# Two-layer graph network: order of the first stage's products, and who fills the gate's bias and the masks into PSUM

## The reference

```
h = relu(layernorm(x))                                   # layer 0, 12 heads of 32
v = h @ W                      ; th = tanh(v)
s = leaky(th . w_src + (th . w_dst)^T, 0.2) ; s = -999 where not adj ; p = softmax(s)
f = elu(p @ v + b)             ; g = sigmoid(h @ H_w.T + H_b)
x = x + g * f + (1 - g) * h
h = relu(layernorm(x))                                   # layer 1, 6 heads of 64
q, k, v = h @ Wq + bq, h @ Wk + bk, h @ Wv + bv
x = x + softmax(q k^T / 8 + (0 or -9e15 by adj)) @ v @ Wf + bf
```

## Time and profile before

| | |
|---|---|
| device time, median of 3 runs | 1072.71 us (1072.68 to 1074.22) |
| the profiled execution's own time | 1072.87 us |
| its span | 1070.8 us |
| busy: PE | 991.1 us (93%), 10153 matmuls |
| busy: DVE | 780.3 us (73%) |
| busy: ACT | 574.5 us (54%) |
| busy: POOL | 277.7 us (26%) |
| chain that ended last | PE 55%, DVE 27%, ACT 7%, issue 7% |

### The profile page before, as it was taken

One profiled execution on the slowest core, in us unless ns is written; L12 is line 12 of the kernel. 1 busy time (PEld: TensorE's weight loads), 2 busy tenths in 40 slices (PEclk: granted clock), 3 DMA queues, 4 the chain that ended last, 5 costly groups with the idle time before them and its releaser, 6 DMA issues.

```text
span 1070.8 us, 24885 instructions
## 1 busy us (share of the span) xinstructions
PE 991.1 (93%) x10153; PEld 857.0 (80%) x10153; DVE 780.3 (73%) x1456; ACT 574.5 (54%) x1126; POOL 277.7 (26%) x338
## 2 busy tenths in 40 slices
PE   6589999999999999999999999999999999999686
PEld 5487878888787887978788797878879788887575
DVE  4867867778786777868677886767788676876814
ACT  6556466373746636374564638446463754745331
POOL 2233140502415051240504124050321406032120
PEclk9689999999999999999999999999999999999988
DMA  9211151510414142031413204151241515111102
GB/s 237 32 15 20 29 90 32 90 32 31 61 32 91 31 82 40 31 62 32 91 32 77 41 12 83 31 91 31 65 39 19 91 32 90 32 47 18 28 30 59
DMA packets 183652, 56.41 MB, mean 53 GB/s; under 512 B 164978, under 2 KB 183540, under 8 KB 183540
## 3 DMA queue, kind: packets, MB, share of 16 engines
q1 hardware_dynamic: 183540, 54.83, 28.3%
HBM read 17.06 MB, written 12.58 MB: 28 GB/s over the span
## 4 chain that ended last, share of the span: by engine, by line
PE 55%; DVE 27%; ACT 7%; issue 7%; POOL 0%; ACTq 0%; DVEq 0%; POOLq 0%
PE ps L624 11%; PE ps L610 10%; PE ps L626 10%; PE ps L625 10%; DVE x L948 5%; PE ps L693 5%; PE ps L790 4%; DVE ee L945 4%; ACT p L430 3%; DVE hT1l L1056 3%; DVE hT0l L858 3%; DVE stats L842 3%; DVE p L973 2%; PE ps L808 2%; DVE x_in L996 2%
## 5 line engine op out<-in xcount | busy, mean ns | idle before, releaser
L410 POOL TENSOR_TENSOR x_in<-x_in,ee 128x384 f32<-128x384 f32 x64 | 72.5, 1134 | 626.7 <-DVE ee L951 626.7
L469 ACT ACTIVATE th<-ps 128x384 f32<-128x384 f32 x64 | 31.9, 499 | 209.8 <-DVE v_tok L936 209.8
L1020 DVE TENSOR_TENSOR hT1l<-ps,hT1h 128x512 fp32r<-128x512 f32 x48 | 30.4, 685 | 88.2 <-ACT hT1h L540 88.1
L984 DVE COPY_PREDICATED_SCALAR z<-not_adj,masked 128x768 f32 x64 | 69.4, 1084 | 32.5 <-ACT z L501 32.5
L610 PE MATMUL ps<-ident,p 128*128 128x128 f32 x576 | 76.3, 283 | 17.8 <-ACT p L430 10.0
L403 POOL TENSOR_TENSOR x_in<-x_in,h 128x384 f32<-128x384 f32 x64 | 85.5, 1367 | 18.5 <-DVE Wf_lo L883 18.5
L610 PEld LDWEIGHTS ps<-ident,p 128*128 128x128 f32 x576 | 65.3, 144 | 23.0 <-issue 12.7
L624 PE MATMUL ps<-Wf_hi,hT1h 128*128 128x384 f32 x192 | 69.0, 359 | 10.4 <-DVE hT1l L1056 10.4
L397 POOL TENSOR_TENSOR x_in<-x_in,bf_row 128x384 f32<-128x384 f32 x64 | 62.1, 1003 | 48.0 <-ACT p L430 48.0
L507 ACT ACTIVATE z<-z 128x768 f32<-128x768 f32 x64 | 54.5, 853 | 28.1 <-DVE z L989 28.0
L501 ACT ACTIVATE z<-ps 128x384 f32<-128x384 f32 x128 | 52.5, 497 | 31.0 <-PE ps L693 31.0
(11 more groups left out here) (130 smaller groups left out, 2796.5 us busy)
## 6 DMA issues: line engine op xcount, KB each, us to landing
V<-v_tok SPq DMA_DIRECT2D x128, 192.0 KB, 5.0
x_in<-in_x_dram SPq DMA_DIRECT2D x16, 768.0 KB, 5.0
out_dram<-x_in SPq DMA_DIRECT2D x16, 768.0 KB, 3.6
x<-in_L_gnn_H_w_dram SPq DMA_DIRECT2D x1, 576.0 KB, 5.9
QT<-in_L_gnn_W_dram SPq DMA_DIRECT2D x3, 192.0 KB, 6.7
thT<-in_L_gnn_Wq_dram SPq DMA_DIRECT2D x1, 576.0 KB, 5.8
z<-in_L_gnn_Wk_dram SPq DMA_DIRECT2D x1, 576.0 KB, 6.8
z<-in_L_gnn_Wv_dram SPq DMA_DIRECT2D x1, 576.0 KB, 7.9
```

The source lines that it names most:

```text
L410: pool.tensor_tensor(x_in[:, i % 3, t], x_in[:, i % 3, t], ee[:, t], ALU.subtract).then_inc(x2_made, 1)
L984: dve.copy_predicated(zt, not_adj[:, t].unsqueeze(1).broadcast_to((P, HEADS0, N)), masked0[:].unsqueeze(2).broadcast_to((P, HEADS0, N))).t ...
```

## The change

- RING begins with the four th_made jobs, then the four gate_tanh jobs, so W0's four products stand in banks 0 to 3 and the gate's in banks 4 to 7. PE makes all W0 products first, then all gate products.
- From i = 2 on ACT copies the broadcast bias (a new tile hb_all, loaded by a new DMA) into the gate's banks, and PE accumulates on it, without the bias matmul.
- In i = 1 to 15 ACT copies the masks into the score banks, and PE's mask matmuls are gone.
- DVE's values0 of the next group move from the head of an iteration to the end of the one before, between the closing steps; those of group 0 stand ahead of the loop, with the late weights' low parts between them. add_out(0) moves ahead of close(2), add_out(1) ahead of close(3).
- ACT's th_and_gate is split, and normalise1 has three th and gate pairs ahead of it instead of two, with the last gate tanh behind it.

```diff
-        pairs_of_jobs = zip(jobs("th_made", 0, th_made, 4), jobs("gate_tanh", 0, gate_tanh, 4))
         RING = (
-            [x for pair in pairs_of_jobs for x in pair]
+            jobs("th_made", 0, th_made, 4)
+            + jobs("gate_tanh", 0, gate_tanh, 4)
...
+        def bias_by_act(i):
+            return real(i) and real(i - 2)
+        def mask_by_act(i):
+            return real(i) and real(i - 1)
...
+            sp.dma_start(hb_all[:], H_b.rearrange("(a e) -> a e", a=1).broadcast_to((P, D))).then_inc(consts_loaded, 16)
...
+                def put_bias(t):
+                    if bias_by_act(i):
+                        act.wait_ge(*last_reader(i, job("gate_tanh", t)))
+                        act.activation(ps[:, job("gate_tanh", t) % BANKS, 0:D], hb_all[:], ACT.Copy).then_inc(bias_put, 1)
+                def put_mask(q):
+                    if mask_by_act(i):
+                        pair = q // 2
+                        act.wait_ge(mask1_made, j + 1)
+                        act.wait_ge(*last_reader(i, job("scores1_shifted", q)))
+                        act.activation(ps[:, job("scores1_shifted", q) % BANKS, 0:D].rearrange("p (t k m) -> p t k m", t=2, m=N),
+                                       mask1[:, 2 * pair:2 * pair + 2].unsqueeze(2).broadcast_to((P, 2, PAIRS1, N)), ACT.Copy)\
+                            .then_inc(mask_put, 1)
...
                     for t in range(TILES):
                         toks = slice(t * P, (t + 1) * P)
                         take(i, job("th_made", t))
+                        if not real(j) and t == TILES - 1:
+                            pe.wait_ge(small_ready, 3)
                         product(ps[:, job("th_made", t) % BANKS, 0:D], lambda c: hT0h[:, c, toks], lambda c: hT0l[:, c, toks],
                                 lambda c: wh["W0"][:, c], lambda c: wl["W0"][:, c]).then_inc(values0_full, 1)
-                        take(i, job("gate_tanh", t))
+                    for t in range(TILES):
+                        toks = slice(t * P, (t + 1) * P)
                         dst = ps[:, job("gate_tanh", t) % BANKS, 0:D]
+                        if bias_by_act(i):
+                            pe.wait_ge(bias_put, TILES * (i - 2) + t + 1)
+                            product(dst, lambda c: hT0h[:, c, toks], lambda c: hT0l[:, c, toks],
+                                    lambda c: wh["Hw"][:, c], lambda c: wl["Hw"][:, c], begun=True).then_inc(gate_full, 1)
+                        else:
...
                 def scores(pair):
+                    if mask_by_act(i):
+                        pe.wait_ge(mask_put, TILES * j + 2 * pair + 2)
...
                 if real(j):
-                    pe.wait_ge(mask1_made, j + 1)
-                    masks()
+                    if not mask_by_act(i):
+                        pe.wait_ge(mask1_made, j + 1)
+                        masks()
```

More of the change, by code:

```diff
@@ L519, in exp_elu @@
                         act.activation(ee[:, t], x1[:, t], ACT.Exp, bias=minus1[:]).then_inc(elu_exp, 1)
-                th_and_gate(0)
-                th_and_gate(1)
+                put_bias(0)
+                tanh_values(0)
+                put_bias(1)
+                tanh_values(1)
+                tanh_gate(0)
+                put_bias(2)
+                tanh_values(2)
+                tanh_gate(1)
+                put_bias(3)
+                tanh_values(3)
+                tanh_gate(2)
                 if real(j):
                     normalise1(j)
-                th_and_gate(2)
-                th_and_gate(3)
+                tanh_gate(3)
                 if real(i):
@@ L568, in body @@
                 copy_k(2)
+                for q in range(4):
+                    put_mask(q)
                 exp0(3)
@@ L617, in take, with product @@
                 return ps[:, at % BANKS]
[L619 removed]
+            def product(dst, left_h, left_l, right_h, right_l, more=False, begun=False, chunk_ready=None):
                 for c in range(C):
@@ L623, in product @@
                         pe.wait_ge(*chunk_ready(c))
-                    pe.matmul(dst, left_h(c), right_h(c), start=(c == 0), stop=False)
-                    pe.matmul(dst, left_h(c), right_l(c), start=False, stop=False)
-                    mm = pe.matmul(dst, left_l(c), right_h(c), start=False, stop=(c == C - 1 and not more))
+                    pe.matmul(dst, left_h(c), right_h(c), start=(c == 0 and not begun), stop=False, skip_group_check=begun)
+                    pe.matmul(dst, left_h(c), right_l(c), start=False, stop=False, skip_group_check=begun)
+                    mm = pe.matmul(dst, left_l(c), right_h(c), start=False, stop=(c == C - 1 and not more), skip_group_check=begun)
                 return mm
@@ L902, in source_dest_consts, with values0 @@
                 dve.wait_ge(sd_consts, 2)
+            def values0(g, t):
+                if real(g):
+                    dve.wait_ge(values0_full, TILES * g + t + 1)
+                    if g == 0 and t == 0:
+                        dve.wait_ge(small_ready, 5)
+                    if real(g - 2) and t == 0:
+                        dve.wait_ge(values1_spread, 64 * (g - 1))
+                    dve.tensor_tensor(v_tok[:, t].rearrange("p (h e) -> p h e", e=E0),
+                                      ps[:, job("th_made", t) % BANKS, 0:D].rearrange("p (h e) -> p h e", e=E0),
+                                      b0_plus1[:].unsqueeze(1).broadcast_to((P, HEADS0, E0)), ALU.add)\
+                        .then_inc(values0_made, 1)
+            for t in range(TILES):
+                values0(0, t)
+                late_lows(t)
+            source_dest_consts()
             def body(i, par):
@@ L1062, in body @@
                 close(1)
+                add_out(0)
                 close(2)
-                add_out(0)
+                values0(i + 1, 0)
+                add_out(1)
+                values0(i + 1, 1)
                 close(3)
-                add_out(1)
                 stats_of_x2(0)
@@ L1069, in body @@
                 add_out(2)
+                values0(i + 1, 2)
                 stats_of_x2(2)
@@ L1074, in body @@
                 add_out(3)
+                values0(i + 1, 3)
             iterations(dve, body)
```

51 lines of the change are left out of this document (16 added, 35 removed).

## The result

| | before | after |
|---|---|---|
| device time, median of 4 runs | 1073.06 us (1072.68 to 1074.22) | 1047.21 us (1046.33 to 1047.84) |
| the profiled execution, its span | 1072.87 us, 1070.8 us | 1046.33 us, 1044.4 us |
| busy: PE | 991.1 us (93%), 10153 matmuls | 968.0 us (93%), 10037 matmuls |
| busy: DVE | 780.3 us (73%) | 775.1 us (74%) |
| busy: ACT | 574.5 us (54%) | 630.1 us (60%) |

The ratio is 0.9757 (0.974 to 0.9774). The changed kernel is 25.9 us faster, where 23.4 were forecast for the medians; 1049.3 had been predicted for it, in a range of 1044 to 1060.

What follows compares the result with a forecast made beforehand. TensorE, busy 60.77 of 63.06 us per iteration, was taken as the bound, waiting mainly for ACT behind the gate's products. 15 x (0.81 + 0.70) + 1.0 - 0.1 = 23.55 us off 1072.87 gave 1049.3, range 1044 to 1060.

Steps and rivals of the forecast that it cites:

- A: Stage from W0's products to Wq's, i = 1 to 15: thT copies come earlier, 0.81 us saved per iteration.
- The copy into PSUM: Price of one ScalarE copy of bias or mask into PSUM: 0.45 us, ends 0.37 and 0.60.
- B: Scores, i = 1 to 15: removing the four mask matmuls that hold PE saves 0.70 us per iteration, ends 0.55 and 0.75.
- C: Start and end: iteration 0's dst_rows comes sooner, 1.0 us gained; close(3) in the last pass gives -0.1.
- Sum: Whole kernel: 15 x (0.81 + 0.70) + 1.0 - 0.1 = 23.55 us saved.
- R1: Rival, first stage: GpSimd's subtractions hold DVE's inserted PSUM readers, A is -0.32, 1066.3 us; chance 0.12 with milder forms.
- R2: Rival, attend1: V1's spread binds if it lands at 555.3, B shrinks to 0.2, 1056.8 us; chance 0.08.
- R3: Rival: ScalarE's copies into PSUM are slow; at 1.5 us each A and B are gone, 1072 us; chance 0.05.
- R4: Rival: PE's new waits among thin work lower the granted clock, making the kernel slower, 1082 us; chance 0.05.

Runs made afterwards that it cites:

- e3: The changed kernel with the gate's bias back as TensorE matmuls in all iterations: 1049.02 us.
- e4: The changed kernel with the gate's bias back on TensorE and values0 of group 1 on back at the head of the iteration: 1058.5 us.
- e5: The changed kernel with ScalarE's tanh of gate tile 3 moved from behind normalise1 to behind the second hT1h copy: 1042.7 us.
- e7: The changed kernel with add_out(0) behind close(2) again instead of ahead of it, one execution: 1052.01 us.
- e6: The changed kernel with each ScalarE bias and mask copy into PSUM made twice, the second waiting for the first: 1048.6 us.
- e2: The kernel before, with only the masks of i = 1 to 15 copied by ScalarE: 1064.04 us.
- e10: The changed kernel with values0 of group 1 on back at the head of the iteration, bias still copied by ScalarE, one execution: 1110.54 us.
- e1: The changed kernel run again without any edit: 1046.94 us.
- e8: The changed kernel with V1's spread cut to a 24th behind group 0, leaving attend1 stale values: 1046.99 us.

## Why the prediction held, step by step

- **A, 0.81 predicted, 1.06 measured.** The mechanism was right: e3, e4 and e5 show that the chain through the row sums and ACT sets Wq's start, that of PE's 0.69 us of saved matmuls 0.20 count there, and that a tanh behind normalise1 costs nearly its length. The size was off in one term. The prediction took GpSimd's subtraction of tile 1 at the 1.27 us of the earlier trace rows; it took 1.02, so close(2)'s first instruction ended at 507.89 in the frame of before, not 508.14, and the sums came 0.70 late instead of 0.93. e7 brings the 1.27 back by moving one instruction. That 1.06 is also the upper bound of the working is chance: the bound let normalise1 wait for tanh_gate(2), and in the trace it waits 0.21 us for the shift. The rest of the schedule came as laid out: gate products end at 517.91 (517.90), the fourth bias copy ends at 516.16 (516.35) and PE doesn't wait for it.
- **The copy into PSUM, 0.45 predicted** from the exps of the earlier trace rows: 0.50 alone, 0.46 from start to start. The Trainium skill, ScalarE: Activation LUTs, "What ACT_TABLE_LOAD costs", gave 0.41 as an estimate; the measurement decides, 0.05 above it. By e6 neither would have changed the sum.
- **B, 0.70 predicted, 0.67 measured** (e2: 0.67 alone). Mask copies at once behind copy_k(2), four in 1.75 us (1.8), and exp0(3) behind them, with nothing late for it.
- **C, 1.0 predicted for the start, 0.98 measured.** dst_rows of iteration 0 starts at 34.16, where 34.1 was worked out from the earlier trace rows, and it waits for PE's wsd products as foreseen:

```profile
34.16 0.46 ACT L583 ACTIVATE dst_rows<-ps,is_dst_src 128x128 f32<-128x128 f32 x1 [1.02 <-PE ps L753]
```

DVE's constants (is_dst_src) came at 32.73 instead of 34.83, 2.1 us sooner and not the 4 of the prediction, which didn't matter. That two single executions hit the forecast so well is partly luck: the first th transpose of iteration 0 starts anywhere from 30.84 (before) to 32.1 (e10). Counted from it, dst_rows comes after 4.25 us before and in e2, and after 3.29 in every kernel with the new order, so the order itself is worth 0.96.
- **Sum, 23.55 predicted, 26.3 of span measured.** Split at the same four places, the prediction had 1.0 for the start, 0.81 for the turn to iteration 1 (A alone), 14 x 1.51 = 21.1 for the periods, 0.6 for the end (B less 0.1); measured were 0.98, 1.31, 22.87 and 1.15. The periods give 14 x 0.22 = 3.1 more than forecast, which is A's 0.25 less 0.03 of B, and lose 1.3 again to waits of attend1 that the prediction did not have. The 1.31 isn't all A's. e2 has the old order up to there, and the same stretch takes 46.65 in it, 47.68 before and 46.37 in the changed kernel: two executions with the same order differ by 1.0. The granted clock goes with it, 0.63 in the mean between dst_rows and the first close of iteration 0 before, 0.68 in e2 and in the changed kernel. Against e2 the turn gave 0.3, less than the 0.81 of A; no run takes that apart. At the end the 1.15 says little, since e1, the same kernel, and e3 to e10 have 102.8 to 105.9 us there (103.15 in the changed kernel, 104.30 before).
- **R1 fell.** values0 takes 0.55 us beside a subtraction (496.51) and alone (500.95), and the two-input instruction of 494.28 is held, to 0.41 us after GpSimd's end. By the rule of the Trainium skill cited in the prediction (SBUF — State Buffer, "Who interferes with whom"), the trace agrees on both halves.
- **R2 is there, but small.** The spread of V1 ends last in two iterations, by at most 0.3 us each (0.6 in all in the profiled execution, 0.7 in e1's), and e8, which removes it, moves the median by nothing measurable. The margin was 0.06 only for the worst landing: in iteration 8 the last issue is at 535.8, the slowest of the four takes 4.7, so it has landed by 540.5, and attend1 starts at 541.36.
- **R3 fell:** e6 doubles the copies and loses 1.4 us, not the gain.
- **R4 did not happen** in the changed kernel (1.00 in the middle; waits of 0.61 and 0.44 us), but e10 shows the mechanism and its price.

## What to carry to other kernels

Before counting matmuls on a 93% busy TensorE, find for each stage what the next product waits for: 9.7 us of bias matmuls were worth 2.1, another order of the products, the tanhs and values0 15 (1064.04 to 1049.02, the sooner start included), and moving one group of three copies from the late engine to an idle one another 16.5. Work moved onto an engine is nearly free while it ends before the semaphore that the engine would wait for anyway (here up to about twice its size), so lay out that engine's row by start-to-start pitches and look for the slack in its bracket. Moving a producer late behind such copies is dear twice, by the wait and by the clock after it.

## What the runs showed of the hardware

- GpSimd's subtraction of 128x384 takes 1.02 us or 1.20 to 1.27, by what DVE starts just ahead of it: 1.27 behind an instruction with two SBUF inputs (495.82 in e7; 1.20 for tile 0's subtraction, also behind one), 1.02 behind one that reads PSUM (493.81) or bn_stats with its one SBUF input (499.56). This holds in nearly every iteration of the traces.
- After one PE wait of 2.84 us the granted clock fell to 0.77 and 0.67 in the next two stretches of 3 us in one iteration and stayed at 1.00 in the one before. The same wait has two prices. Over e10's 14 periods each us at the lower level went with 0.46 us lost.
- Within attend1's 96 small matmuls PE's sequencer pauses for 0.2 to 0.8 us in some iterations, most of them among the first five, at a place that moves by five or six instructions per iteration and is the same in the changed kernel, e1, e7 and e8.
